# Attention's order and copy engines, and the queues of the feed-forward loads, in a transformer layer on 8 cores

## The chip, the cores and the metric

One Trainium2 chip, all 8 NeuronCores. Each core has TensorE (PE, matmuls), VectorE (DVE), ScalarE (ACT), GpSimd and SyncE (SP); SP and ACT also issue DMAs. The metric is the device time in microseconds (us) of the slowest core for the whole kernel. Each core computes its own 1024 rows of the result, with no exchange between cores.

## The reference

Attention with 16 query heads and 4 key/value heads, RMS-normed q and k, a causal mask, residual and layer norm, then a gated feed-forward layer, again with residual and layer norm. x is (2, 4096, 2048) in fp32, the hidden size is 8192.

```python
q = (x @ Wq).reshape(b, s, 16, 128)
k = (x @ Wk).reshape(b, s, 4, 128)
v = (x @ Wv).reshape(b, s, 4, 128)
q = _rmsnorm(q, q_gamma); k = _rmsnorm(k, k_gamma)      # k, v repeated for 4 heads each
scores = einsum('bqhd,bkhd->bhqk', q, k) * 128 ** -0.5   # causal mask
out = einsum('bhqk,bkhd->bqhd', softmax(scores), v).reshape(b, s, 2048) @ Wo
y = _layernorm(x + (out + x))
gate = einsum('bsd,hd->bsh', y, w_gate)
up = einsum('bsd,hd->bsh', y, w_up)
z = einsum('bsh,dh->bsd', silu(gate) * up, w_down)
result = _layernorm(y + z)
```

## The kernel before

A core takes one of the two sequences and every fourth tile of 128 rows of it, 8 tiles in all (NT = 8, slot g). The kernel runs in stages: K and V of all 4096 positions, Q of the core's rows, attention, output projection with layer norm, feed-forward, last layer norm. Engines run their own queues in program order and wait for each other by semaphores (`wt` is a wait, `tick` an increment; `sch` and `vch` also make the engine wait for its own instruction).

**Attention.** There are 8 x 16 iterations i, one for each slot g and head h. Slot g sees nb = g + 1 chunks of 512 keys. An iteration has four parts:

- `emit_stats(i)`: for each chunk one score matmul on PE into one of two PSUM tiles `pss` (L426), copied by ACT into `scr` (L432).
- `emit_sm_front(i)`: DVE masks the last chunk (L441) and takes the row maximum of all of them (L444).
- `emit_sm_back(i)`: ACT takes exp over all chunks into `ph`, with the row sum (L457); DVE takes the reciprocal (L462) and scales `ph` (L463).
- `emit_tav(i)`: for each chunk q4, PE transposes four blocks of `ph` into one of two tiles `pst` (L484), an engine EV copies them to `pt4` (L501 on ACT, L505 on DVE), and PE multiplies them with V into `pso` (L512). EV is ACT for even i and DVE for odd i. The transposes of chunk q4 + 1 are emitted ahead of the copy of q4, and the copy waits for them (L498); behind the last chunk stands a dummy transpose (L497). At the end EV copies `pso` into `zT` (L522, L526).

The loop emits front(i+1), back(i), stats(i+2), tav(i); ahead of it stand stats(0), stats(1) and front(0). At the first head of a slot ACT issues the load of the next slot's mask.

**Feed-forward.** The hidden size is done in 64 steps eht = 8 e8 + ht, eight to a block. A step multiplies the 1024 rows with 128 columns of the gate weights (L740, L743, 32 matmuls) and of the up weights (L750, L753, 32 matmuls). ACT applies SiLU to the gate (L760), DVE multiplies it with up (L764). After eight steps follow 256 down matmuls (L775), added into `f` by DVE (L786).

Weights come in fp32 and are cast. `issue_w(eht)` issues 32 loads of 64 KB, 16 into `wgs32` (L712) and 16 into `wus32` (L716), all from SP, into one of two buffers; SP waits for the cast of two steps before. `issue_w(eht + 1)` is called at the head of step eht. ACT casts both (L733, L734). The down weights of a step, 1 MB, are loaded into the single buffer `wds` (L730), issued by ACT, and cast by DVE into `wd16` (L767) behind the multiplication. The head of a step in the kernel before:

```python
if eht + 1 < 64:
    issue_w(eht + 1)
wt(SE, ve, wd_cast)
wd_rd = swd.tick(
    SE.dma_start(wds[:], wdT_d[128 * eht:128 * (eht + 1), :]))
wt(SE, swgu[p], w_rd[p])
wt(SE, te, w16_used[p])
SE.copy(wgs16[p][:], wgs32[p][:])
w_cast[p] = se.tick(SE.copy(wus16[p][:], wus32[p][:]))
```

Of the kernel before, what the change touches and what calls it, by code (L numbers as in the profile page):

```python
# [34 lines left out]
def build_program():  # L35
# [25 lines left out]
    def wt(eng, sem, val):  # L61
        if val <= 0:
            return
        key = (id(eng), id(sem))
        if wait_memo.get(key, 0) < val:
            eng.wait_ge(sem.h, val)
            wait_memo[key] = val
# [13 lines left out]
    with ExitStack() as ctx0:  # L81
        e0 = ctx0.enter_context
        te = Sem(nc, ctx0, "te")
        ve = Sem(nc, ctx0, "ve")
# [20 lines left out]
        with ExitStack() as ctxY, ExitStack() as ctxZ, ExitStack() as ctxA:  # L105
# [282 lines left out]
            with ExitStack() as c3:  # L388
# [29 lines left out]
                def emit_stats(i):  # L418
                    g, h = it_gh(i)
                    nb = g + 1  # L420
                    rho = i % 2
                    g4 = h // 4
                    for kb in range(nb):
                        p = kb % 2
                        wt(TE, se, sc[p])
                        mm = TE.matmul(pss[p][:], qT[:, h, 128 * g:128 * (g + 1)],  # L426
                                       kT[:, g4, 512 * kb:512 * (kb + 1)],
                                       start=True, stop=True)
                        mmd = te.tick(mm)
                        wt(SE, te, mmd)  # L430
                        wt(SE, ve, ve_scr_done[rho])
                        sc[p] = se.tick(SE.copy(scr[rho][:, 512 * kb:512 * (kb + 1)],  # L432
                                                pss[p][:]))

                def emit_sm_front(i):
                    g, h = it_gh(i)
                    nb = g + 1
                    rho = i % 2
                    wt(VE, se, max(sc))
                    wt(VE, sdm[g % 2], dm_ready[g % 2])  # L440
                    vch(VE.tensor_tensor(scr[rho][:, 512 * g:512 * (g + 1)],  # L441
                                         scr[rho][:, 512 * g:512 * (g + 1)],
                                         dmb[g % 2][:], op=OP.min))
                    nm_done[rho] = vch(VE.tensor_reduce(nm[rho][:],  # L444
                                                        scr[rho][:, 0:512 * nb],
                                                        axis=AX, op=OP.max, negate=True))
                    ve_scr_done[rho] = nm_done[rho]
                    dm_used[g % 2] = nm_done[rho]

                def emit_sm_back(i):  # L450
                    g, h = it_gh(i)
                    nb = g + 1
                    rho = i % 2
                    wt(SE, ve, nm_done[rho])
                    wt(SE, ve, li_done[rho])
                    wt(SE, te, te_ph_done[rho])
                    exp_done = sch(SE.activation(ph[rho][:, 0:512 * nb],  # L457
                                                 scr[rho][:, 0:512 * nb],
                                                 ACT.Exp, bias=nm[rho][:],
                                                 accum_out=ell[rho][:]))  # L460
                    wt(VE, se, exp_done)
                    li_done[rho] = vch(VE.reciprocal(li[rho][:], ell[rho][:]))  # L462
                    ex_done[rho] = vch(VE.tensor_scalar(ph[rho][:, 0:512 * nb],  # L463
                                                        ph[rho][:, 0:512 * nb],
                                                        li[rho][:, 0:1], 0.0,
                                                        op0=OP.mult, op1=OP.add))

                def emit_tav(i):
                    g, h = it_gh(i)
                    nb = g + 1  # L470
                    rho = i % 2
                    g4 = h // 4
                    EV = SE if (i % 2 == 0) else VE
                    evs = se if (i % 2 == 0) else ve
                    wt(TE, ve, ex_done[rho])
                    wt(TE, se if zev_eng[rho] == 0 else ve, zev_done[rho])

                    def emit_tchunk(q4):
                        pp = q4 % 2
                        wt(TE, se, se_pt_done[pp] if se_pt_eng[pp] == 0 else 0)  # L480
                        wt(TE, ve, se_pt_done[pp] if se_pt_eng[pp] == 1 else 0)
                        tr = None
                        for u in range(4):
                            tr = TE.transpose(pst[pp][:, 128 * u:128 * (u + 1)],  # L484
                                              ph[rho][:, 512 * q4 + 128 * u:
                                                       512 * q4 + 128 * (u + 1)], id16[:])
                        return te.tick(tr)

                    tch = [0] * (nb + 1)
                    tch[0] = emit_tchunk(0)  # L490
                    av_done = 0
                    for q4 in range(nb):
                        if q4 + 1 < nb:
                            tch[q4 + 1] = emit_tchunk(q4 + 1)
                        else:
                            tch[q4 + 1] = te.tick(
                                TE.transpose(pjk3[:], id16[:], id16[:]))  # L497
                        wt(EV, te, tch[q4 + 1])  # L498
                        if EV is SE:
                            se_pt_done[q4 % 2] = evs.tick(  # L500
                                SE.copy(pt4[q4 % 2][:], pst[q4 % 2][:]))  # L501
                            se_pt_eng[q4 % 2] = 0
                        else:
                            se_pt_done[q4 % 2] = evs.tick(
                                VE.tensor_copy(pt4[q4 % 2][:], pst[q4 % 2][:]))  # L505
                            se_pt_eng[q4 % 2] = 1
                        wt(TE, se if se_pt_eng[q4 % 2] == 0 else ve,
                           se_pt_done[q4 % 2])
                        av = None
                        for u in range(4):  # L510
                            ktile = 4 * q4 + u
                            av = TE.matmul(pso[rho][:],  # L512
                                           vsb[:, ktile, 128 * g4:128 * (g4 + 1)],
                                           pt4[q4 % 2][:, 128 * u:128 * (u + 1)],
                                           start=(ktile == 0),
                                           stop=(ktile == 4 * nb - 1))
                        av_done = te.tick(av)
                    te_ph_done[rho] = te.n
                    wt(EV, te, av_done)
                    if EV is SE:  # L520
                        zev_done[rho] = evs.tick(
                            SE.copy(zT[:, h, 128 * g:128 * (g + 1)], pso[rho][:]))  # L522
                        zev_eng[rho] = 0
                    else:
                        zev_done[rho] = evs.tick(
                            VE.tensor_copy(zT[:, h, 128 * g:128 * (g + 1)], pso[rho][:]))  # L526
                        zev_eng[rho] = 1
# [7 lines left out]
                for i in range(NIT):  # L535
                    g, h = it_gh(i)
                    if h == 0 and g + 1 < NT and dm_issued < g + 1:
                        pn = (g + 1) % 2
                        wt(SE, ve, dm_used[pn])
                        dm_ready[pn] = sdm[pn].tick(  # L540
                            SE.dma_start(dmb[pn][:], dmask_d[g + 1]))
                        dm_issued = g + 1
                    if i + 1 < NIT:
                        emit_sm_front(i + 1)
                    emit_sm_back(i)
                    if i + 2 < NIT:
                        emit_stats(i + 2)
                    emit_tav(i)
            zev_all = se.n
            ctxA.close()  # L550

# [129 lines left out]
            with ExitStack() as c5m:  # L681
# [24 lines left out]
                def issue_w(eht):  # L706
# [3 lines left out]
                    for dc in range(16):  # L710
# [2 lines left out]
                                         wgT_d[128 * dc:128 * (dc + 1),  # L713
                                               128 * eht:128 * (eht + 1)]))
                        r = swgu[p].tick(
                            SY.dma_start(wus32[p][:, dc, :],  # L716
                                         wuT_d[128 * dc:128 * (dc + 1),
                                               128 * eht:128 * (eht + 1)]))
                    w_rd[p] = r
# [2 lines left out]
                for e8 in range(8):  # L722
                    for ht in range(8):
                        eht = 8 * e8 + ht
                        p = eht % 2
                        if eht + 1 < 64:
                            issue_w(eht + 1)
                        wt(SE, ve, wd_cast)
                        wd_rd = swd.tick(
                            SE.dma_start(wds[:], wdT_d[128 * eht:128 * (eht + 1), :]))  # L730
                        wt(SE, swgu[p], w_rd[p])
                        wt(SE, te, w16_used[p])
                        SE.copy(wgs16[p][:], wgs32[p][:])  # L733
# [182 lines left out]
```

How the kernel before makes its waits and increments, by code:

```python
    def tick(self, instr, k=1):  # L29
        self.n += k * self.step
        instr.then_inc(self.h, k * self.step)
        return self.n
# [28 lines left out]
    def wt(eng, sem, val):  # L61
        if val <= 0:
            return
        key = (id(eng), id(sem))
        if wait_memo.get(key, 0) < val:
            eng.wait_ge(sem.h, val)
            wait_memo[key] = val
```

## Time and profile before

| | |
|---|---|
| median of 2 runs | 5664.69 us (5649.74 to 5679.64) |
| profiled execution | 5473.53 us |
| its span, slowest core | 5472.3 us |
| spans of the other cores | 5440.4 to 5465.0 us |
| PE matmul busy | 3427.8 us (63%) |
| ACT busy | 1412.4 us (26%) |
| DVE busy | 1305.9 us (24%) |
| chain that ended last, by engine | PE 58%, ACT 16%, DVE 14% |

All times in the profile are of one execution on the slowest core. "Idle before" a group is the time its engine stood still directly ahead of its instructions, with the instruction that released it. The granted clock is TensorE's, as a share of 2.4 GHz. A DMA's row on SPq or ACTq is its issue on the queue of that engine, not the transfer.

### The profile page before, as it was taken

The numbers are of one execution on the slowest core, as the hardware profiler recorded it, in microseconds if no ns is written. First come the engines' busy times: TensorE is split into PE (matmuls) and PEld (weight loads), VectorE is DVE, ScalarE is ACT, GpSimd is POOL, SyncE is SP. The second block draws the span as 40 slices with busy tenths as digits, with TensorE's granted clock in tenths as the row PEclk, the third lists the DMA queues.
The fourth block names the chain that finished last, engine by engine and source line by source line (L and its number), as shares of the span: only waits on it lengthen the run. The fifth ranks groups of instructions, "written<-read, shape, count | busy, mean of one in ns | idle before, by whom it ended". The sixth has DMA issues, their size and how long they took to land.

```text
span 5472.3 us, 43357 instructions; the slowest of 8 cores (5440.4 to 5472.3 us)
## 1 busy us (share of the span) xinstructions
PE 3427.8 (63%) x15152; PEld 1619.8 (30%) x15152; DVE 1305.9 (24%) x1799; ACT 1412.4 (26%) x2525; POOL 0.2 (0%) x4
## 2 busy tenths in 40 slices
PE   3565567677545555555555435577878788787872
PEld 1222223233222333333333212233323333232331
DVE  1111100000244443334333323111212112121216
ACT  1222211212344444444444301111111111112111
POOL 0000000000000000000000000000000000000000
PEclk8676677888655555555555567788989889898986
DMA  3111121121000000000000030443242423424221
GB/s 110 47 53 54 49 68 46 49 80 48 26 4 3 1 3 2 1 3 1 1 0 1 20 134 31 118 120 106 87 134 87 137 86 103 120 88 137 87 71 62
DMA packets 343077, 325.20 MB, mean 59 GB/s; under 512 B 38224, under 2 KB 300496, under 8 KB 326480
## 3 DMA queue, kind: packets, MB, share of 16 engines
q1 hardware_dynamic: 311760, 177.71, 11.7%
q10 hardware_dynamic: 31104, 144.72, 7.9%
q8 instruction: 126, 2.06, 0.2%
q14 instruction: 87, 0.71, 0.0%
HBM read 313.88 MB, written 8.39 MB: 59 GB/s over the span
## 4 chain that ended last, share of the span: by engine, by line
PE 58%; ACT 16%; DVE 14%; issue 7%; DMA 3%; ACTq 1%; DVEq 0%; SPq 0%
PE psd L775 8%; PE psq L323 8%; PE pso L512 6%; PE psg L740 5%; PE psg L743 5%; PE pst L484 5%; PE psu L753 4%; PE psu L750 4%; ACT pt L501 3%; DVE nm L444 3%; PE psk L221 3%; ACT ph L457 3%; PE psv L223 3%; DVE pt L505 2%; PE pswo L615 2%
## 5 line engine op out<-in xcount | busy, mean ns | idle before, releaser
L740 PE MATMUL psg<-yT,wgs 128*128 128x512 f16 x1024 | 469.1, 458 | 404.6 <-ACT wus L734 404.6
L512 PE MATMUL pso<-pt,vsb 128*128 128x128 f16 x2304 | 336.1, 299 | 432.8 <-ACT pt L501 237.5
L323 PE MATMUL psq<-wqs,xqs 128*128 128x512 f32 x1024 | 486.5, 638 | 44.5 <-DMA xqs<-xqT 40.2
L775 PE MATMUL psd<-wd,gatedT 128*128 128x512 f16 x2048 | 455.0, 386 | 20.9 <-DVE wd L767 20.9
L743 PE MATMUL psg<-yT,wgs 128*128 128x512 f16 x1024 | 466.4, 456 | 0.0
L484 PE MATMUL pst<-id,ph 128*128 128x128 f16 x2304 | 336.3, 310 | 178.8 <-DVE ph L463 178.8
L426 PE MATMUL pss<-kT,qT 128*128 128x512 f16 x576 | 311.1, 604 | 195.9 <-ACT scr L432 194.9
L432 ACT COPY scr<-pss 128x512 f32<-128x512 f32 x576 | 312.4, 587 | 405.0 <-PE pss L426 395.8
L753 PE MATMUL psu<-yT,wus 128*128 128x512 f16 x1024 | 388.2, 379 | 0.0
L750 PE MATMUL psu<-yT,wus 128*128 128x512 f16 x1024 | 388.1, 379 | 0.0
L764 DVE TENSOR_TENSOR gatedT<-gsil,psu 128x1024 f16<-128x1024 f16 x64 | 78.1, 1221 | 1298.1 <-PE psu L753 1298.1
L512 PEld LDWEIGHTS pso<-pt,vsb 128*128 128x128 f16 x2304 | 199.7, 126 | 569.3 <-issue 569.3
L444 DVE TENSOR_REDUCE nm<-scr 128x1 f32<-128x512 f32 (+7 forms) x128 | 326.8, 2553 | 13.9 <-DVE scr L441 0.9
L484 PEld LDWEIGHTS pst<-id,ph 128*128 128x128 f16 x2304 | 254.5, 144 | 233.9 <-issue 231.3
L760 ACT ACTIVATE gsil<-psg 128x1024 f16<-128x1024 f32 x64 | 65.5, 1023 | 958.6 <-PE psg L743 958.6
L323 PEld LDWEIGHTS psq<-wqs,xqs 128*128 128x128 f32 x1024 | 202.5, 204 | 322.7 <-issue 322.1
L740 PEld LDWEIGHTS psg<-yT,wgs 128*128 128x128 f16 x1024 | 117.1, 114 | 596.6 <-issue 522.2
L457 ACT ACTIVATE ph<-scr,nm 128x512 f16<-128x512 f32 (+7 forms) x128 | 283.9, 2218 | 0.0
L775 PEld LDWEIGHTS psd<-wd,gatedT 128*128 128x128 f16 x2048 | 202.8, 99 | 273.1 <-issue 39.9
L501 ACT COPY pt<-pst 128x512 f16<-128x512 f16 x288 | 168.5, 585 | 443.3 <-PE pst L484 373.5
L733 ACT CAST wgs<-wgs 128x2048 f16<-128x2048 f32 x64 | 121.4, 1897 | 568.4 <-DVE wd L767 551.0
L221 PE MATMUL psk<-wkv,xTt 128*128 128x512 f16 x512 | 237.3, 463 | 38.8 <-ACT xTt L211 38.8
(107 smaller groups left out, 2684.5 us busy)
## 6 DMA issues: line engine op xcount, KB each, us to landing
wgs<-wgT SPq DMA_DIRECT2D x1024, 64.0 KB, 2.0
wds<-wdT ACTq DMA_DIRECT2D x64, 1024.0 KB, 4.9
wus<-wuT SPq DMA_DIRECT2D x1024, 64.0 KB, 2.0
xr<-x ACTq DMA_DIRECT2D x32, 1024.0 KB, 5.8
wqs<-wq SPq DMA_DIRECT2D x64, 256.0 KB, 3.1
wqs<-wq ACTq DMA_DIRECT2D x64, 256.0 KB, 3.1
wos<-wo SPq DMA_DIRECT2D x16, 1024.0 KB, 6.4
xqs<-xqT ACTq DMA_DIRECT2D x32, 256.0 KB, 7.9
```

The source lines that it names most:

```text
L221: TE.matmul(psk[p][:], lhsT, wkv[:, dc, 0:512], start=(dc == 0), stop=(dc == 15))
L323: mq = TE.matmul(psq[j][:], xqs[:, dc, 128 * j:128 * (j + 1)], wqs[dc % 2][:], start=(dc == 0), stop=(dc == 15))
L444: nm_done[rho] = vch(VE.tensor_reduce(nm[rho][:], scr[rho][:, 0:512 * nb], axis=AX, op=OP.max, negate=True))
L457: exp_done = sch(SE.activation(ph[rho][:, 0:512 * nb], scr[rho][:, 0:512 * nb], ACT.Exp, bias=nm[rho][:], accum_out=ell[rho][:]))
L484: tr = TE.transpose(pst[pp][:, 128 * u:128 * (u + 1)], ph[rho][:, 512 * q4 + 128 * u: 512 * q4 + 128 * (u + 1)], id16[:])
L501: SE.copy(pt4[q4 % 2][:], pst[q4 % 2][:]))
L512: av = TE.matmul(pso[rho][:], vsb[:, ktile, 128 * g4:128 * (g4 + 1)], pt4[q4 % 2][:, 128 * u:128 * (u + 1)], start=(ktile == 0), stop=(kti ...
L740: mg = TE.matmul(psg[:, 0:512], wgs16[p][:, dc, :], yT[:, dc, 0:512], start=(dc == 0), stop=(dc == 15))
L743: mg = TE.matmul(psg[:, 512:1024], wgs16[p][:, dc, :], yT[:, dc, 512:1024], start=(dc == 0), stop=(dc == 15))
L750: mup = TE.matmul(psu[:, 0:512], wus16[p][:, dc, :], yT[:, dc, 0:512], start=(dc == 0), stop=(dc == 15))
L753: mup = TE.matmul(psu[:, 512:1024], wus16[p][:, dc, :], yT[:, dc, 512:1024], start=(dc == 0), stop=(dc == 15))
L775: md = TE.matmul(psd[:, 512 * dout:512 * (dout + 1)], gatedT[:, ht2, 128 * tt:128 * (tt + 1)], wd16[:, ht2, 512 * dout:512 * (dout + 1)], ...
```

## The change

Three things are changed.

1. In attention the loop emits tav(i-1) at the head of iteration i, ahead of front(i+1), back(i) and stats(i+2), and the last tav behind the loop. A name `rho3` is brought in for the index of `scr`; it is i % 2, as `rho` is.
2. In `emit_tav` the engine that copies a chunk alternates by (i + q4) % 2 instead of by i % 2. The copy into `zT` stays by i % 2.
3. In the feed-forward stage the loads of `wus32` are issued by ACT instead of SP, and the load of `wds` is issued by SP for even eht and by ACT for odd eht.

The diff, without the lines that only rename `rho` to `rho3`:

```diff
@@ emit_sm_front, emit_sm_back, emit_stats @@
+                    rho3 = i % 2
...
@@ emit_tav @@
-                        wt(EV, te, tch[q4 + 1])
-                        if EV is SE:
-                            se_pt_done[q4 % 2] = evs.tick(
+                        EVq = SE if (i + q4) % 2 == 0 else VE
+                        evq = se if (i + q4) % 2 == 0 else ve
+                        wt(EVq, te, tch[q4 + 1])
+                        if EVq is SE:
+                            se_pt_done[q4 % 2] = evq.tick(
                                 SE.copy(pt4[q4 % 2][:], pst[q4 % 2][:]))
                             se_pt_eng[q4 % 2] = 0
                         else:
-                            se_pt_done[q4 % 2] = evs.tick(
+                            se_pt_done[q4 % 2] = evq.tick(
                                 VE.tensor_copy(pt4[q4 % 2][:], pst[q4 % 2][:]))
                             se_pt_eng[q4 % 2] = 1
@@ loop over i @@
                         dm_issued = g + 1
+                    if i >= 1:
+                        emit_tav(i - 1)
                     if i + 1 < NIT:
                         emit_sm_front(i + 1)
                     emit_sm_back(i)
                     if i + 2 < NIT:
                         emit_stats(i + 2)
-                    emit_tav(i)
+                emit_tav(NIT - 1)
@@ issue_w @@
                         r = swgu[p].tick(
-                            SY.dma_start(wus32[p][:, dc, :],
+                            SE.dma_start(wus32[p][:, dc, :],
                                          wuT_d[128 * dc:128 * (dc + 1),
                                                128 * eht:128 * (eht + 1)]))
@@ loop over ht @@
                         if eht + 1 < 64:
                             issue_w(eht + 1)
-                        wt(SE, ve, wd_cast)
+                        Qd = SY if eht % 2 == 0 else SE
+                        wt(Qd, ve, wd_cast)
                         wd_rd = swd.tick(
-                            SE.dma_start(wds[:], wdT_d[128 * eht:128 * (eht + 1), :]))
+                            Qd.dma_start(wds[:], wdT_d[128 * eht:128 * (eht + 1), :]))
```

## Rows read from the trace of the kernel before

**Rows 1.** Stretches: us, then busy PE, PEld, DVE, ACT, POOL; clock, DMA share, GB/s.

```profile
1414.00:3121.00 1707.00, 887.37 (x5267) 510.10 (x5267) 675.07 (x863) 794.19 (x1244) 0.00 (x0) 0.50 0.01 2
3454.60:5361.00 1906.40, 1481.27 (x6148) 632.40 (x6149) 327.12 (x384) 303.39 (x194) 0.00 (x0) 0.87 0.36 106
```

**Rows 2.** Costliest groups: busy us, mean ns | idle before, released by.

```profile
L740 PE MATMUL psg<-yT,wgs 128*128 128x512 f16 x1024 | 469.1, 458 | 404.6 <-ACT wus L734 404.6
...
L457 ACT ACTIVATE ph<-scr,nm 128x512 f16<-128x512 f32 (+7 forms) x128 | 283.9, 2218 | 0.0
...
L733 ACT CAST wgs<-wgs 128x2048 f16<-128x2048 f32 x64 | 121.4, 1897 | 568.4 <-DVE wd L767 551.0
```

**Rows 3.** Timelines of ACT, PE, DVE, one feed-forward step: start us, us, instruction [idle before].

```profile
3976.56 1.02 ACT L760 ACTIVATE gsil<-psg 128x1024 f16<-128x1024 f32 x1 [9.38 <-PE psg L743]
...
3982.99 0.38 PE L753 MATMUL psu<-yT,wus 128*128 128x512 f16 x1
...
3984.61 1.22 DVE L767 CAST wd<-wds 128x2048 f16<-128x2048 f32 x1
...
3986.34 1.90 ACT L733 CAST wgs<-wgs 128x2048 f16<-128x2048 f32 x1 [8.76 <-DVE wd L767]
...
3990.18 0.58 PE L740 MATMUL psg<-yT,wgs 128*128 128x512 f16 x1 [6.82 <-ACT wus L734]
```

**Rows 4.** Chain that ended last, attention, g = 7: start us, us, what.

```profile
2788.83 0.59 ACT pt L501
...
2790.66 0.59 ACT pt L501
...
2801.34 0.59 ACT pt L501
...
2802.91 3.81 ACT ph L457 x2
...
2812.43 0.44 DVE pt L505
...
2814.11 0.44 DVE pt L505
...
2825.39 0.69 DVE scr L441
...
2832.48 0.58 PE pst L484 x4
```

**Rows 5.** Timelines of PE and DVE in the same stretch.

```profile
2811.26 1.06 PE L484 MATMUL pst<-id,ph 128*128 128x128 f16 x8
...
2823.93 0.42 DVE L505 COPY pt<-pst 128x512 f16<-128x512 f16 x1 [0.94 <-PE pjk L497]
```

**Rows 6.** Groups by shape in attention, nb = 2.

```profile
L444 DVE TENSOR_REDUCE nm<-scr 128x1 f32<-128x1024 f32 x16 | 19.5, 1220 | 1.6
...
L457 ACT ACTIVATE ph<-scr,nm 128x1024 f16<-128x1024 f32 x16 | 18.5, 1156 | 0.0
```

**Rows 7.** Timeline of SP's queue, feed-forward: first and last of 14 issues.

```profile
3975.69 0.43 SPq L712 DMA_DIRECT2D wgs<-wgT  x1
...
3981.86 0.43 SPq L716 DMA_DIRECT2D wus<-wuT  x1
```

**Rows 8.** Timeline of ACT and its queue, K/V stage and Q stage.

```profile
86.38 0.27 ACT L258 COPY kT<-ptk 128x128 f16<-128x128 f16 x1 [1.46 <-PE pjk L254]
86.46 0.33 ACTq L185 DMA_DIRECT2D xr<-x  x1
...
1091.41 9.07 ACTq L309 DMA_DIRECT2D xqs<-xqT  x15
```

**Rows 9.** Stretches as in rows 1: a gate, start of down matmuls, Q stage.

```profile
4013.55:4023.30 9.75, 9.75 (x33) 3.82 (x34) 0.00 (x0) 0.00 (x0) 0.00 (x0) 0.70 0.46 127
4125.11:4128.50 3.39, 3.39 (x9) 1.19 (x10) 0.00 (x0) 3.02 (x2) 0.00 (x0) 0.51 0.66 213
849.00:904.00 55.00, 54.73 (x104) 23.03 (x104) 0.00 (x0) 0.00 (x0) 0.00 (x0) 0.81 0.21 62
```

More of the change, by code:

```diff
@@ L420, in emit_stats @@
                     nb = g + 1
-                    rho = i % 2
+                    rho3 = i % 2
                     g4 = h // 4
@@ L430, in emit_stats @@
                         wt(SE, te, mmd)
-                        wt(SE, ve, ve_scr_done[rho])
-                        sc[p] = se.tick(SE.copy(scr[rho][:, 512 * kb:512 * (kb + 1)],
+                        wt(SE, ve, ve_scr_done[rho3])
+                        sc[p] = se.tick(SE.copy(scr[rho3][:, 512 * kb:512 * (kb + 1)],
                                                 pss[p][:]))
@@ L438, in emit_sm_front @@
                     rho = i % 2
+                    rho3 = i % 2
                     wt(VE, se, max(sc))
                     wt(VE, sdm[g % 2], dm_ready[g % 2])
-                    vch(VE.tensor_tensor(scr[rho][:, 512 * g:512 * (g + 1)],
-                                         scr[rho][:, 512 * g:512 * (g + 1)],
+                    vch(VE.tensor_tensor(scr[rho3][:, 512 * g:512 * (g + 1)],
+                                         scr[rho3][:, 512 * g:512 * (g + 1)],
                                          dmb[g % 2][:], op=OP.min))
                     nm_done[rho] = vch(VE.tensor_reduce(nm[rho][:],
-                                                        scr[rho][:, 0:512 * nb],
+                                                        scr[rho3][:, 0:512 * nb],
                                                         axis=AX, op=OP.max, negate=True))
-                    ve_scr_done[rho] = nm_done[rho]
+                    ve_scr_done[rho3] = nm_done[rho]
                     dm_used[g % 2] = nm_done[rho]
@@ L453, in emit_sm_back @@
                     rho = i % 2
+                    rho3 = i % 2
                     wt(SE, ve, nm_done[rho])
@@ L457, in emit_sm_back @@
                     exp_done = sch(SE.activation(ph[rho][:, 0:512 * nb],
-                                                 scr[rho][:, 0:512 * nb],
+                                                 scr[rho3][:, 0:512 * nb],
                                                  ACT.Exp, bias=nm[rho][:],
```

## Prediction

> **What bounds the kernel now.** I read the table of stretches first [rows 1]. Attention (1414 to 3121 us) is 1707 us with PE busy 887 and the granted clock at 0.50 throughout (1.2 GHz); no engine is near full, so a chain of dependent steps sets it. The feed-forward stage is 1906 us with PE busy 1481: matmuls set it, and the holes between them. Next the costliest groups [rows 2]: the largest hole is L740, the first gate matmul, which sat 404.6 us behind the ACT cast of L734. ACT's first cast (L733) in turn sat 551.0 us behind the DVE cast of L767.
>
> The timelines of one feed-forward step say why [rows 3]. Count from the start of SiLU, 3976.56. Up matmuls end at 3982.99 + 0.38 = 3983.37 (+6.81). DVE multiplies, then casts wds until 3984.61 + 1.22 = 3985.83 (+9.27). ACT has waited for that, because its next instruction is the load into wds. It issues it, casts from 3986.34 (+9.78), and the next gate starts at 3990.18 (+13.62), 6.82 after the up matmuls. The hole stands before ht = 1 to 7 of each block, 56 times; the weights of ht = 0 are cast under the down matmuls.
>
> In attention I followed the chain of waits over a pair of iterations at g = 7 [rows 4]. The even one repeats: ACT copy, four AV matmuls, four transposes, next ACT copy, 1.83 us apart (2788.83, 2790.66). The odd one does the same with DVE, 1.68 apart (2812.43, 2814.11). Between them I count from the end of the last copy. After the even one (2801.34 + 0.59 = 2801.93) exp starts 0.98 later, since the zT copy after the AV matmuls is ahead of it on ACT; then come exp and the score copies and matmuls, and the next transposes start at 2811.26 [rows 5]: 9.33. After the odd one (2823.93 + 0.42 = 2824.35 [rows 5]) DVE's mask starts at 2825.39, then reduction and scale, and the next transposes at 2832.48: 8.13. These two ways are 8.35 from exp's start and 7.09 from the mask's.
>
> **The change, part by part.** *Renaming.* rho3 equals rho; the same instructions come out. Nothing.
>
> *Moving emit_tav.* Before, iterations run front(i+1), back(i), stats(i+2), tav(i); after, tav(i-1), front(i+1), back(i), stats(i+2). Written out, these are one sequence cut at another place, with the last tav added behind the loop. Every engine's order stays. Only the load of dmask, 8 in all, goes ahead of a tav on ACT's queue, in front of a copy that waits for transposes anyway; a single issue took 0.33 [rows 8]. At most 8 x 0.33 = 3 us if it were not hidden; I take nothing.
>
> *Alternating the copies.* The copy of chunk q4 waits for the transposes of q4 + 1, and the transposes of q4 + 2 are queued on PE behind the AV matmuls of q4, which wait for that copy. So two copies never overlap, whichever engines do them. A pair of iterations still holds as many ACT as DVE pitches, 3.51 for two. Bounds: all 448 pitches behind a first chunk at 1.68, or all at 1.83, in place of their mean: -33 to +33 us; I take 0.
>
> What loses its cover is the rest: exp ran under odd iterations (their copies were DVE's), DVE's mask and reduction under even ones. Both now come behind the copies. For nb = 8: the odd iteration's last copy is now ACT's, and its zT copy is DVE's, so exp starts at once and ACT's way ends 8.35 after the copy, DVE's old way 8.13: 0.22 longer. The even iteration's last copy is now DVE's, which starts the mask at once: 7.09, hidden under ACT's 9.33 by 2.2. At smaller even nb ACT's way shrinks faster than DVE's after odd iterations; at odd nb the engine in question has its last copy a chunk earlier. The barest cover is after even ones at nb = 2, where exp + 0.85 must outlast reduction + 0.72: 1.16 + 0.85 = 2.01 against 1.22 + 0.72 = 1.94 [rows 6]. Sum: 8 x 0.22 = +2 us.
>
> *wds by turns from SP and ACT.* For even eht ACT no longer waits for DVE; for odd eht it does. Even steps with a hole are ht = 2, 4, 6 in 8 blocks: 24; odd ones 32. SP's wait for wd_cast stands behind its 16 loads of wgs(eht+1), which have been issued by then, and ahead of those of wgs(eht+2), which can't start before this step's casts anyway. The load starts at the same moment as now and is wanted a whole step later. Nothing late.
>
> *wus from ACT.* This decides. ACT now issues 16 DMAs between SiLU and the casts, in every step. No row shows 64 KB loads in a run on ACT. SP's start 6.17 / 13 = 0.474 apart (first and last of 14) [rows 7]. ACT's loads of xqs are 9.07 / 15 = 0.605 apart [rows 8], but they are 256 KB each, 433 GB/s, where the transfers could be the limit; SP's run at 138 GB/s. I take 0.474; the range keeps 0.605. A DMA starts while ACT computes, 0.08 after the start of a copy [rows 8]. So the 16 run from +0.10 to 0.10 + 16 x 0.474 = +7.7. Odd steps: ACT then waits until +9.27 as before; this costs nothing and has 1.6 us to spare (issues up to 0.573). Even steps: the casts start at +7.7 instead of +9.78, 2.1 us each: 24 x 2.1 = -50 us. SP's own 16 start with the gate and end 7.6 later, before ACT's. By the Trainium skill (Advanced Engine Details and Errata, "Clock Domains") the SP and ACT sequencers run at one clock; by that ACT's pitch is SP's and the sum is the same. No run here shows it yet.
>
> The Trainium skill (DMA: Bandwidth & Descriptors, "Issuing engines are not separate DMA queues") says that starting DMAs on several engines saves only the time to start them, usually small. By that rule alone the move of wus would change nothing. Here the issues are 15.2 us a step on SP, where they are hidden, and the half that moves to ACT takes most of what the freed wait gives.
>
> *Clock.* A gate behind a hole begins at 0.50; the one at 4013.55 had 0.70 over 9.75 us for what the up matmuls do in 6.9 [rows 9], so up to 2.9 lost. The hole of even steps falls to 4.7 us. A hole of 2.61, before the down matmuls at 4125.11, was followed by 0.51 too, so I take no gain. Bound: 24 x 2.9 = -70.
>
> *Start of the stage.* ACT issues 32 DMAs ahead of its first cast where SP issued 32 whose landing it awaited: nothing.
>
> **Sum.** 5472.3 - 50 + 2 = 5424 for the span of this execution. It took 5473.53 in all; the median of the two runs is 5664.69, 191 longer. The trace shows a level of 0.81 under long matmul stretches [rows 9]. At it the 6.9 us of up matmuls become 8.5, the wait for DVE ends 1.6 later, and an even step gains 3.7: 89 us in all. How much of the 191 is that isn't shown; between 50 and 89 I take 65: 5664.7 - 65 = 5600 us.
>
> **Rivals.**
> *A. ACT issues slower.* For: the xqs loads [rows 8]. Against: they are four times as large. At 0.605 an even step gains nothing and the casts of an odd one come 0.4 later: 32 x 0.4 = +14, 5679 us; each 0.05 more costs 16 x 56 x 0.05 = 45. Over 2% (113 us) from 0.72. Chance 0.10.
> *B. Slower, attention.* The exp of odd iterations, once hidden, adds to the gap behind them: half of 283.9 [rows 2] = +142, less the 65: 5742 us. It decides where exp and score copies outlast DVE's way by more than a little. Against: the reduction is as long as exp or longer from nb = 2 on [rows 6], and the mask comes on top. Chance 0.07.
> *C. The whole hole goes* in 24 steps, the issues being so short (under 0.2) that issues and casts fit under the up matmuls: 24 x (6.8 + 2.9) = -233: 5432 us. Against: the pitch of rows 7. Chance 0.05.
> *D. Copies on two engines overlap*, and a pitch falls by a copy's 0.5: 448 x 0.5 = -224: 5441 us. Against: PE's order, above. Chance 0.04.
>
> **How the numbers follow.** The forecast, a gain of about 1%, has 0.74. A measurement of this kernel tells about 2% from no change: 5551 to 5778. Faster takes C, D and 0.01 of the forecast's low side: 0.10. Slower takes the far parts of A and B, where issues pass 0.72 or both costs add up: 0.10. Same: 0.80. The low end, 5555, has most of the clock's 70 or the 33 of attention; the high end, 5690, has 0.605 on ACT, or +33 with nothing from 0.81.
>
> **What would show it.** ACT's queue behind SiLU: 16 issues, 0.474 apart, the last done at +7.7. The hole before the gate: 4.7 us for ht = 2, 4, 6, and 6.8 for the odd. L733 waits for L767 only 32 times. In attention the same starts of chunks and gaps, with exp no longer under the copies. It is wrong if ACT's pitch differs, if the gate's slow stretch goes, or if a gap in attention moves by over 1 us.

## The result, and the profile after

| | before | changed |
|---|---|---|
| median | 5591.84 us (5451.77 to 5737.63, 10 runs) | 5514.41 us (5388.62 to 5669.48, 11 runs) |
| ratio | | 0.9883, 95% interval 0.9835 to 0.993 |

The kernel became 1.2% faster. The forecast said a gain of about 1% (5600 / 5664.69 = 0.9886), by the mechanism that the profile then showed, but gave it as 5600 us, from 5555 to 5690, and the time measured is 5514.

In some executions of either kernel some cores are granted a clock of 0.81 in long matmul stretches and the kernel takes up to 5% longer; the ratio above and, unless it is said otherwise, the stage times below leave these out.

Attention is cut here from the first score matmul to the first load of the output projection's weights, feed-forward from the first load of `wgs32` to the first transpose of the last layer norm. In the profiled execution of the changed kernel core 3 kept the full clock in both (span 5394.1 us). Its stretches of attention and of feed-forward, columns as in [rows 1]:

```profile
1413.20:3115.20 1702.00, 891.98 (x5312) 515.14 (x5312) 671.49 (x864) 783.59 (x1185) 0.00 (x0) 0.50 0.01 2
...
3431.00:5282.60 1851.60, 1476.38 (x6145) 630.43 (x6146) 327.17 (x384) 303.66 (x193) 0.00 (x0) 0.89 0.38 109
```

Cut at the same instructions, the kernel before has 1700.0 us of attention and 1906.1 of feed-forward on its core 0 (its eight cores: 1699.6 to 1701.2, and 1906.1 to 1909.6). So on these cores attention took 2 us more and feed-forward 54.5 less. The waits of the feed-forward stage (engine, line, waited for: us in total, times, longest) name the holes, which are the times PE stands still ahead of a gate. They came to 404.6 us [rows 2] and are now 354.8. Where ACT had waited 551.0 us for DVE alone [rows 2], there are now 32 waits for DVE and 32 in which it waited for nothing but its own queue:

```profile
PE psg L747 <- ACT wus L741: 354.8, 57, 20.7
ACT wgs L740 <- DVE wd L774: 277.6, 32, 9.0
...
ACT wgs L740 <- issue: 224.6, 32, 15.4
```

And the timeline of ACT and its queue over an even and an odd step:

```profile
3939.20 1.03 ACT L767 ACTIVATE gsil<-psg 128x1024 f16<-128x1024 f32 x1 [9.32 <-PE psg L750]
3939.22 7.73 ACTq L722 DMA_DIRECT2D wus<-wuT  x16
3947.04 1.90 ACT L740 CAST wgs<-wgs 128x2048 f16<-128x2048 f32 x1 [6.81 <-issue]
3948.85 1.89 ACT L741 CAST wus<-wus 128x2048 f16<-128x2048 f32 x1
3959.79 1.02 ACT L767 ACTIVATE gsil<-psg 128x1024 f16<-128x1024 f32 x1 [9.05 <-PE psg L750]
3959.81 7.54 ACTq L722 DMA_DIRECT2D wus<-wuT  x16
3969.09 0.34 ACTq L737 DMA_DIRECT2D wds<-wdT  x1
3969.52 1.90 ACT L740 CAST wgs<-wgs 128x2048 f16<-128x2048 f32 x1 [8.71 <-DVE wd L774]
```

The 16 issues begin 0.02 us after the start of SiLU and last 7.5 to 7.7 us in most steps (9.1 at most). In the even step the first cast follows them, 7.84 after SiLU here (7.7 in most); in the odd step ACT is through with them after 7.56 and then waits for DVE until 9.3, as in [rows 3].

### The profile page after: what moved, and what is told of

Its sections match the earlier page's. It is cut to its first block, busy times and chain, and to the rows that moved or that the text cites. A ratio compares the mean times of both kernels' runs of the same rounds, so it can differ in the third digit from the quotient of the medians.

```text
span 5554.5 us, 43304 instructions; the slowest of 8 cores (5394.1 to 5554.5 us)
## 1 busy us (share of the span) xinstructions
PE 3590.1 (65%) x15152; PEld 1656.2 (30%) x15152; DVE 1300.9 (23%) x1799; ACT 1413.6 (25%) x2525; POOL 0.2 (0%) x4
## 4 chain that ended last, share of the span: by engine, by line
PE 57%; ACT 17%; DVE 13%; issue 7%; ACTq 4%; DMA 2%; DVEq 0%; SPq 0%
PE psd L782 10%; PE psq L323 8%; PE psg L747 6%; PE pso L516 6%; PE psg L750 6%; PE pst L486 5%; ACT ph L459 4%; ACTq L722 3%; PE psu L760 3%; PE psu L757 3%; ACT pt L505 3%; PE psk L221 3%; PE psv L223 3%; DVE nm L445 2%; PE pswo L621 2%
## 5 line engine op out<-in xcount | busy, mean ns | idle before, releaser
L747 PE MATMUL psg<-yT,wgs 128*128 128x512 f16 x1024 | 493.5, 482 | 328.0 <-ACT wus L741 328.0
L782 PE MATMUL psd<-wd,gatedT 128*128 128x512 f16 x2048 | 533.0, 433 | 20.9 <-DVE wd L774 20.9
L750 PE MATMUL psg<-yT,wgs 128*128 128x512 f16 x1024 | 490.7, 479 | 0.0
L323 PE MATMUL psq<-wqs,xqs 128*128 128x512 f32 x1024 | 461.1, 612 | 38.2 <-DMA xqs<-xqT 37.2
L760 PE MATMUL psu<-yT,wus 128*128 128x512 f16 x1024 | 432.4, 422 | 0.0
L757 PE MATMUL psu<-yT,wus 128*128 128x512 f16 x1024 | 432.3, 422 | 0.0
L782 PEld LDWEIGHTS psd<-wd,gatedT 128*128 128x128 f16 x2048 | 220.8, 108 | 333.2 <-issue 293.9
L509 DVE COPY pt<-pst 128x512 f16<-128x512 f16 x288 | 122.3, 425 | 821.2 <-PE pst L486 658.2
```

Of the source, the lines that this page charges most:

```text
L323: mq = TE.matmul(psq[j][:], xqs[:, dc, 128 * j:128 * (j + 1)], wqs[dc % 2][:], start=(dc == 0), stop=(dc == 15))
L747: mg = TE.matmul(psg[:, 0:512], wgs16[p][:, dc, :], yT[:, dc, 0:512], start=(dc == 0), stop=(dc == 15))
L750: mg = TE.matmul(psg[:, 512:1024], wgs16[p][:, dc, :], yT[:, dc, 512:1024], start=(dc == 0), stop=(dc == 15))
L757: mup = TE.matmul(psu[:, 0:512], wus16[p][:, dc, :], yT[:, dc, 0:512], start=(dc == 0), stop=(dc == 15))
L760: mup = TE.matmul(psu[:, 512:1024], wus16[p][:, dc, :], yT[:, dc, 512:1024], start=(dc == 0), stop=(dc == 15))
L782: md = TE.matmul(psd[:, 512 * dout:512 * (dout + 1)], gatedT[:, ht2, 128 * tt:128 * (tt + 1)], wd16[:, ht2, 512 * dout:512 * (dout + 1)], ...
```

## Experiments: which part made the difference

Stage times, us, each kernel on one core at the full clock. Cores of one execution differ by 2 to 4 us in attention and, in the kernels with regular holes, by up to 3.5 us in feed-forward; with wds always from SP they differ by 14 us or more:

| kernel | attention | feed-forward |
|---|---|---|
| before | 1700.0 | 1906.1 |
| changed | 1702.0 | 1851.6 |
| feed-forward part alone | 1701.4 | 1851.6 |
| attention part alone | 1702.5 | 1909.7 |
| wus from ACT alone | 1700.5 | 1902.7 |
| wds by turns alone | 1699.4 | 1691.1 |
| whole change, wus issued behind the casts | 1701.2 | 1684.3 |
| whole change, wus as one DMA | 1702.5 | 1687.7 |
| wds always from SP | 1699.5 | 1458.6 |
| same, one DMA each for wgs and wus | 1701.9 | 1380.1 |
| transposes one chunk further ahead | 1262.4 | 1906.2 |
| same, copies alternating | 1266.7 | 1909.5 |

**The feed-forward part alone.** The attention of before, the queues of the change.

```diff
-                            SY.dma_start(wus32[p][:, dc, :],
+                            SE.dma_start(wus32[p][:, dc, :],
...
-                        wt(SE, ve, wd_cast)
+                        Qd = SY if eht % 2 == 0 else SE
+                        wt(Qd, ve, wd_cast)
```

> The change without its attention part: wus from ACT, wds by turns, attention as before. My theory: all of the gain is here. ACT's first cast starts 7.7 us after SiLU in even steps and 9.7 in odd ones, the hole before the gate is 4.7 us for ht = 2, 4, 6 and 6.8 for ht = 1, 3, 5, 7; the feed-forward stage falls from 1906 us to 1850 to 1875, the ratio to before is 0.988 to 0.992, as for the whole change. Rival, that the attention part brings some of it: a ratio nearer to 0.995.

Feed-forward took 1851.6 us on seven cores and 1855.0 on one, the same as in the whole change. The whole times (5389.24 to 5549.8 us in 4 runs, before 5593.91 to 5787.73 in 7) spread too widely for the ratio that was expected. The stage carries the verdict: all the gain is here.

**The attention part alone.** The reverse.

> The change without its feed-forward part. My theory: the moved tav is the same sequence and the copies never overlap, so the attention stage takes 1702 us instead of 1700 (0.2 us more for each of 8 pairs at nb = 8), ratio 1.000. Rival B, exp loses its cover: attention 1840 us, ratio 1.025. Rival D, copies overlap: attention near 1475 us, ratio 0.96.

```profile
1397.60:3100.10 1702.50, 892.84 (x5312) 515.87 (x5312) 671.58 (x864) 782.24 (x1185) 0.00 (x0) 0.50 0.01 2
```

This stretch is attention on core 2: 1702.5 us, and 1700.8 to 1702.9 over the eight cores, against 1699.6 to 1701.2. Rivals B and D are out. From the starts of DVE's reductions, a pair of iterations takes 23.48 us at nb = 4 and 34.11 at nb = 6 in both kernels, and at nb = 8 44.9 instead of 44.7 in the mean of the cores. That is the 0.2 of the sum.

The stage alone would not show so little: kernels with the attention of before reach 1702.3 us on single cores. Cut in two it does. The time from the start of the first to that of the last copy into `pt4`, summed over the 128 iterations, is 752.5 us before and 752.1 here; the rest of the stage is 948.0 and 949.6. That rest lies between 947.7 and 948.3 us on every core of the six kernels with the old attention, and between 949.3 and 950.1 with the changed one. So the copies cost the same, and what lost its cover costs 1.6 us.

**wus from ACT alone.**

> Only the loads of wus go to ACT; wds stays on ACT in every step. My theory: the 16 issues end 7.7 us after SiLU, before DVE's cast at 9.27, so they are hidden in all steps: casts start at 9.7 to 9.8, holes 6.8, feed-forward 1906 us, ratio 1.000. Rival, that fewer issues on SP bring loads earlier and with them time: feed-forward below 1890. Rival A, that issues on ACT are dear: casts later than 9.8 and feed-forward above 1920.

1902.7 us on cores 4 to 7, with casts 9.8 us after SiLU and holes of 6.8 in nearly all steps. That is 3.4 us less than before. Of it 1.3 is a shorter wait before the first gate of the stage (21.3 us instead of 22.6); the rest was not followed up, and cores of the kernel before differ by as much (1906.1 and 1909.6). Under DVE's wait the 7.6 us of issues are hidden.

**wds by turns alone.** wus stays on SP.

> Only wds goes by turns; wus stays on SP. My theory: without 16 issues between SiLU and the casts ACT casts about 1 us after SiLU's start in even steps, done 4.9 after it, under the 6.8 us of up matmuls, so the hole before ht = 2, 4, 6 is gone and with it the gate's slow start: 24 x (6.8 + 2.5) = 220 us, feed-forward near 1690 us, ratio 0.96. Then the move of wus costs the change some 160 us of what the freed wait gives. Rival: SP's 32 issues (15.2 us) behind its wait for DVE bring the weights late, and the hole only changes its releaser: feed-forward above 1800, ratio 0.98 or more.

ACT's timeline on core 6, an even step and the next SiLU, and the stretch of the stage:

```profile
3922.50 1.02 ACT L761 ACTIVATE gsil<-psg 128x1024 f16<-128x1024 f32 x1 [9.80 <-PE psg L744]
3923.42 1.89 ACT L734 CAST wgs<-wgs 128x2048 f16<-128x2048 f32 x1
3925.21 1.90 ACT L735 CAST wus<-wus 128x2048 f16<-128x2048 f32 x1
3936.36 1.02 ACT L761 ACTIVATE gsil<-psg 128x1024 f16<-128x1024 f32 x1 [9.26 <-PE psg L744]
```

```profile
3414.70:5105.80 1691.10, 1430.32 (x6144) 621.80 (x6145) 327.11 (x384) 299.97 (x193) 0.00 (x0) 0.90 0.41 120
```

The casts follow SiLU at once, the hole is gone, and so is the slow start of the gate: SiLU to SiLU is 13.86 us here and 23.24 in the step before (from 3899.26). 1906.1 - 1691.1 = 215 us, as worked out (220). So wds by turns is worth 215 us, and wus from ACT, ahead of the casts, takes 160 of it away again (1851.6 - 1691.1).

**The same 16 loads behind the casts.** The whole change, with the issues at another place:

```diff
+                def issue_wu(eht):
...
                         w_cast[p] = se.tick(SE.copy(wus16[p][:], wus32[p][:]))
+                        if eht + 1 < 64:
+                            issue_wu(eht + 1)
```

> The whole change, but ACT issues the 16 loads of wus for the next step behind the two casts of a step instead of ahead of them. My theory: it is only their place between SiLU and the casts that costs. Casts of even steps start 0.9 us after SiLU, the holes of ht = 2, 4, 6 go, feed-forward 1691 us as with wus on SP; attention 1702. Rival, that 1024 more DMAs on ACT cost wherever they stand: feed-forward above 1750.

ACT and its queue on core 4:

```profile
3910.00 5.77 ACTq L727 DMA_DIRECT2D wus<-wuT  x12
3921.59 1.02 ACT L775 ACTIVATE gsil<-psg 128x1024 f16<-128x1024 f32 x1 [9.81 <-PE psg L758]
3921.77 0.82 ACTq L727 DMA_DIRECT2D wus<-wuT  x2
3922.51 1.89 ACT L746 CAST wgs<-wgs 128x2048 f16<-128x2048 f32 x1
3922.61 1.90 ACTq L727 DMA_DIRECT2D wus<-wuT  x4
...
3924.55 4.80 ACTq L727 DMA_DIRECT2D wus<-wuT  x10
```

1684.3 us. The 16 issues of the step are 2 + 4 + 10; those of the step before ended at 3915.77. The first two, at 3921.77, run while SiLU computes and the casts that stand ahead of them in the program have not started. So ACT's queue went on to the DMAs without waiting for those casts to start. With the same DMAs on the same queue the stage takes 1851.6 us when they stand in front of the casts and 1684.3 when they stand behind them: it is their place. One thing was not foreseen: the kernel beats wus on SP (1691.1) by 7. Of this 6 are at the start of the stage, where the wait before the first gate is 15.8 us instead of 22.0.

**One DMA in place of 16.** The whole change, at the old place:

```diff
-                    for dc in range(16):
...
+                    r = swgu[p].tick(
+                        SE.dma_start(wus32[p][:],
+                                     wuT_d[:, 128 * eht:128 * (eht + 1)].rearrange(
+                                         "(c p) n -> p c n", p=128)))
```

> The whole change, but the 16 loads of wus of a step are one DMA of 1 MB from ACT, at the same place. My theory: one issue holds ACT for 0.4 us instead of 7.6, casts of even steps start 1 us after SiLU, feed-forward near 1691 us. Rival, that a long DMA holds the queue that issues it for several us (as the wus issues from SP did, 4 to 6 us each, when they came right behind a wgs of 1 MB): casts of even steps later than 4 us after SiLU, feed-forward above 1720.

ACT on core 1:

```profile
3904.94 1.02 ACT L767 ACTIVATE gsil<-psg 128x1024 f16<-128x1024 f32 x1 [9.36 <-PE psg L750]
3904.95 0.37 ACTq L722 DMA_DIRECT2D wus<-wuT  x1
3905.86 1.89 ACT L740 CAST wgs<-wgs 128x2048 f16<-128x2048 f32 x1
```

One issue of 1 MB, in 2048 rows of 512 bytes, took 0.37 us (the median of 64 as well), no more than one of 64 KB; feed-forward 1687.7 us (1691.1 on others). What cost the 160 us was the number of DMAs issued there. A long DMA right behind another is a different case, as the kernel with one DMA each for wgs and wus shows below.

## Experiments: how far the two ideas go

**wds always from SP**, wus on SP too (`Qd = SY`).

> As wds by turns, but wds comes from SP in every step, wus from SP too; attention as before. My theory: the wait of ACT for DVE was all that made the holes. All 56 go, and SP's queue becomes the bound of a step: 32 issues at 0.474 and one for wds are 15.6 us against 13.8 of gate and up matmuls. Feed-forward 8 x (57.1 + 2.6) + 8 x 13.8 + 56 x 15.7 + 20 = 1487 us, so 1460 to 1520 on an undisturbed die. Rival, that SP behind its wait for DVE falls back further and weights come late: above 1560, with holes of 3 us or more.

ACT on core 0, and the stretch of the stage:

```profile
4035.65 1.02 ACT L761 ACTIVATE gsil<-psg 128x1024 f16<-128x1024 f32 x1 [9.20 <-PE psg L744]
4038.07 1.90 ACT L734 CAST wgs<-wgs 128x2048 f16<-128x2048 f32 x1 [1.39 <-DMA wus<-wuT]
...
4049.47 1.02 ACT L761 ACTIVATE gsil<-psg 128x1024 f16<-128x1024 f32 x1 [7.70 <-PE psg L744]
4053.96 1.90 ACT L734 CAST wgs<-wgs 128x2048 f16<-128x2048 f32 x1 [3.47 <-DMA wus<-wuT]
```

```profile
3417.90:4876.50 1458.60, 1358.33 (x6145) 604.82 (x6146) 329.43 (x384) 301.07 (x193) 0.00 (x0) 0.97 0.48 139
```

1458.6 us (1451.1 to 1466.0 over the cores), less than the 1487 expected and just under the low end given, 1460. From the second block on the holes of ht = 1 to 4 are gone; from ht = 5 the casts wait for the loads, and holes of 0 to 3.5 us come back (1.9 to 2.8 in the median). SP is the bound only in the second half of a block, since what it issued under the down matmuls carries the first half; the sum had charged it in all steps.

**The same with one DMA each for wgs and wus.**

> As wds from SP, and the 16 loads of wgs of a step are one DMA of 1 MB, those of wus another (same 512-byte rows): 2 issues instead of 32. My theory: if the cost is per issue, SP is free and a step is bound by its matmuls, 13.8 us: feed-forward 8 x 59.7 + 64 x 13.8 + 20 = 1381 us where the clock stays at 1.00. Rival, that the cost is per row described (2048 rows of 512 bytes in each DMA either way): one issue lasts about 7.6 us and the stage takes as long as with 32, near 1487.

```profile
3422.20:4802.30 1380.10, 1342.14 (x6145) 603.66 (x6146) 327.13 (x384) 297.51 (x193) 0.00 (x0) 0.98 0.56 147
```

SP's queue on the same core, one step:

```profile
3623.48 0.34 SPq L730 DMA_DIRECT2D wds<-wdT  x1
3623.91 0.39 SPq L711 DMA_DIRECT2D wgs<-wgT  x1
3624.34 4.00 SPq L715 DMA_DIRECT2D wus<-wuT  x1
```

1380.1 us against 1381 worked out, with PE busy for 1342; the six cores at the full clock lie between 1376.2 and 1390.4, so the agreement to 1 us is chance. A second DMA of 1 MB right behind the first does hold its queue: 4.0 us here, 6.3 in the median of the 64 and 11.4 at most. On SP nothing urgent stands behind it. So the issue of a large DMA is short only where no other large one stands directly ahead of it; what the second waits for isn't shown.

**Transposes one chunk further ahead.** The attention of before, with a third `pst`; in `emit_tav` the transposes of q4 + 2 come ahead of the AV matmuls of q4, and the copy into `pt4` waits for the AV matmuls of q4 - 2:

```diff
+                    emit_next(0)
+                    emit_next(1)
...
                     for q4 in range(nb):
-                        if q4 + 1 < nb:
-                            tch[q4 + 1] = emit_tchunk(q4 + 1)
...
+                        emit_next(q4 + 2)
```

> The kernel before with a third pst tile: the transposes of chunk q4 + 2 go ahead of the AV matmuls of q4 on PE, so the copy of q4 + 1 need not wait for those of q4; copies stay on one engine per iteration. My theory: PE's order was what kept the copies apart. A pitch falls from 1.76 to 0.9 to 1.0 us (four transposes and four AV matmuls at 1.2 GHz are 0.86), 448 x 0.8 = 360 us, attention near 1340 us. Rival: the copy and its waits bound a pitch in any order, attention above 1600 us.

The chain in an even iteration at g = 7, and the stretch of attention:

```profile
2555.08 0.58 PE pso L522 x4
2555.66 0.43 PE pst L484 x4
2556.09 0.43 PE pso L522 x4
2556.52 0.43 PE pst L484 x4
...
2558.87 0.59 ACT pt L512
```

```profile
1404.80:2667.20 1262.40, 734.51 (x5312) 465.89 (x5312) 674.27 (x864) 776.37 (x1185) 0.00 (x0) 0.69 0.01 2
```

In the middle of the iteration the copies have left the chain: PE goes from AV to transposes without a wait, 0.86 us a chunk. The first copy and the last two are still in it. The stage took 438 us less, more than the 360 expected. From copy to copy the chunks took 752 us in all before and 332 here, or 1.68 and 0.74 each (core 0); the rest of the stage gives 17. 0.74 is less than the 0.86 that four transposes and four AV matmuls take at 1.2 GHz: the expectation had priced PE at that level throughout, and the granted clock rose from 0.50 to 0.69. How the surplus divides between the clock and the order isn't shown.

**The same, copies alternating.**

> As the kernel with the third pst tile, but copies alternate between ACT and DVE by (i + q4) % 2 as in the change. My theory: PE already bounds a pitch with one engine, so alternating gains nothing more here either, and exp and DVE's reduction lose their cover: attention within 1340 to 1370 us, equal to or up to 20 us over the kernel with one engine. Rival D in this order: two engines overlap their copies, attention 40 us or more below that kernel.

```profile
1394.20:2660.90 1266.70, 747.43 (x5312) 468.21 (x5312) 671.46 (x864) 785.43 (x1185) 0.00 (x0) 0.66 0.01 2
```

1263.8 to 1267.7 us over the cores against 1262.4 to 1265.8, or 2 us more in the mean. The expected level was missed as in the last kernel, the comparison held, but not only for the reason given. From copy to copy the chunks take 322 us in the mean of the cores, 10 less than with one engine (333), so PE was not all of the bound there. The rest of the stage takes 944 us instead of 931: exp and DVE's reduction lose their cover. The two cancel.

**Together.** Third `pst`, wds from SP, one DMA each for wgs and wus.

> What helped, together: the third pst tile with transposes one chunk further ahead (copies on one engine per iteration), wds from SP, wgs and wus as one DMA each from SP. My theory: the stages don't touch each other, so attention 1263 us and feed-forward 1380 us stay, 4475 us on an undisturbed die, ratio to before 0.82. Rival: the longer busy stretches lower the clock (0.81) and feed-forward is above 1440 on all cores, ratio 0.84 or more.

Core 3, and the feed-forward stretch of core 0:

```profile
1399.40:2659.80 1260.40, 731.01 (x5312) 463.72 (x5312) 674.17 (x864) 775.94 (x1185) 0.00 (x0) 0.69 0.01 2
...
2973.30:4349.60 1376.30, 1336.72 (x6144) 602.63 (x6145) 327.04 (x384) 297.07 (x193) 0.00 (x0) 0.99 0.56 147
```

```profile
2983.60:4405.10 1421.50, 1345.08 (x6145) 602.11 (x6146) 327.48 (x384) 300.69 (x193) 0.00 (x0) 0.98 0.55 142
```

Median 4517.6 us (4485.78 to 4755.96, 4 runs), with 5635.31 (5449.2 to 5775.73, 7 runs) for before beside it. The lowest times of both give 0.823, without an interval. On core 3 the two gains add up as expected (span 4461.4 us, where 4475 was worked out). The other cores took 4485.8 to 4516.8, with up to 45 us more in feed-forward at nearly the same clock. On core 0 the casts of ht = 4 to 7 come up to 6.4 us after SiLU, 3.7 in the mean, instead of 0.9. They wait for the weights: 39 waits for the loads of wus, 126.6 us in all, against 7 and 25.9 on core 3, and from issue to landing such a load takes 21.4 us in the median against 15.7. So here the arrival of the weights bounds these steps; why they are slower on one core than on another isn't shown.

## Why the prediction was right and where it was wrong

**The moved tav and the renaming: right.** They were put at nothing, and the kernel with the attention part alone leaves nothing for them beside the 1.6 us below. They were not run by themselves.

**Alternating: right.** +2 us worked out for what loses its cover, +1.6 measured as the rest of the stage, and 0 for the copies, where 752.5 us became 752.6 (means of the eight cores). The chain of the changed kernel on core 3 shows the pitches mixed, 3.52 us for one of ACT and one of DVE, where [rows 4] give 1.83 + 1.68:

```profile
2811.96 0.60 ACT pt L505
...
2813.81 0.44 DVE pt L509
...
2815.48 0.60 ACT pt L505
```

The experiments with a third `pst` confirm the reason, PE's order: with that order changed the copies drop out of most of the chain, and only then do two engines gain on the copies (10 us).

**wds by turns and wus from ACT: right.** Even casts come at +7.7 and odd ones at +9.7, and the pitch is 7.54 / 16 = 0.47 on ACT as on SP. That agrees with the one clock that the Trainium skill (Advanced Engine Details and Errata, "Clock Domains") gives for both sequencers. The holes are 4.7 us before most of ht = 2, 4, 6 and 6.8 before the others. The sum was 50 us; the shorter holes of the even steps gave 48.3. The stage gave 54.5, since two terms that the prediction put at nothing were small gains: 1.9 at the start of the stage (22.6 us before the first gate, now 20.7), and 3.7 in the gates, which from first gate matmul to SiLU took 592.7 us in all before and 589.0 after. Cores 0 and 1 show 1872.6 us; core 0 had 0.81 in place of 1.00 in the last 150 us of the stage. Rival A is out, by the pitch of 0.47 (why the xqs loads stood 0.605 apart isn't shown), and so is C, by the 7.7 us. What C priced at 233 us was had at 215 as soon as the issues stood elsewhere.

The Trainium skill's rule that starting DMAs on several engines saves only the starting time (DMA: Bandwidth & Descriptors, "Issuing engines are not separate DMA queues") agrees with the kernel with wus from ACT alone, which changed 3.4 us. The starting time is paid by the engine that gets it; in front of the casts that was 160 us here.

**The clock: right.** Behind the holes of 4.7 us the gates take 8.8 to 9.5 us, behind those of 6.8 they take 9.1 to 9.9, and behind no hole 7.2. So the slow start stayed, as the prediction said. Behind shorter holes it is not certain: with wds from SP, on core 0, one hole of 2.34 us was followed by the full clock and another by 0.52.

**The saving at 0.81: right in kind.** On core 6, which had 0.81 for most of this stage, the odd step casts at +11.23 and the even one at +7.69, a gain of 3.5 us where 3.7 was worked out. The 89 us for all even steps have no counterpart, since the trace of before has no core with this level in the stage. The steps on core 6:

```profile
3959.30 1.02 ACT L767 ACTIVATE gsil<-psg 128x1024 f16<-128x1024 f32 x1 [11.10 <-PE psg L750]
...
3970.53 1.90 ACT L740 CAST wgs<-wgs 128x2048 f16<-128x2048 f32 x1 [10.20 <-DVE wd L774]
...
3984.45 1.02 ACT L767 ACTIVATE gsil<-psg 128x1024 f16<-128x1024 f32 x1 [10.23 <-PE psg L750]
...
3992.14 1.90 ACT L740 CAST wgs<-wgs 128x2048 f16<-128x2048 f32 x1 [6.67 <-issue]
```

**The step that failed** is the first term of the last sum, "5664.7 - 65 = 5600". Every saving was set against 5664.69, the median of two runs. Over ten runs the median of before is 5591.84, 73 us less, and single ones lie between 5451.77 and 5737.63. The working had seen that the profiled execution was 191 us shorter than that median, and had put that down in part to the level of 0.81. It used this to raise the saving from 50 to 65 us, but not to ask how often the level comes, nor to widen the range: its ends, 5555 and 5690, held only the doubts about the change. Those doubts were the small part. The forecast's ratio on the base that was measured later gives 0.9886 x 5591.84 = 5528, and 5514.41 is within 0.3% of it. That closeness is in part luck: 15 of the 65 us stand for the level of 0.81, and the measured ratio of 0.9883 leaves such executions out. For the others the working gives 5424 / 5472.3 = 0.991, also inside the interval. And the base moves with the executions that happen to be drawn: three later sets of before (7, 3 and 7 executions) have medians of 5635.8, 5636.1 and 5635.3 us, on which the forecast's ratio gives some 5571, inside the range. A range that took in the profiled 5473 as a possible base, less 50, would have started at about 5420 and held the result. How much of the two first runs was that level can't be said, as they have no record of the clock; that it can go with 190 us is shown by the cores of one execution (wus from ACT alone), die 0 with it and die 1 without (cores 0 to 3 are die 0). Of the 200 us between cores 3 and 4, 82 are in feed-forward (1985.1 and 1902.7 us):

```profile
core 3: 5624.9 us, clock 0.683
core 4: 5424.8 us, clock 0.718
```

## What to carry to other kernels

A DMA issued by a compute engine costs that engine its issue time, so count the issues between a release and the work that waits, and put them behind that work or make them one large DMA (not two in a row); the same 16 loads cost 160 us in one place and nothing in another. A wait for another engine's result in front of a load holds all that is queued behind it: moving the load to a queue with nothing urgent behind it was the whole gain here. When two engines share a chain of short steps, look first for the program order on the third engine that keeps the steps apart, because dividing them brings nothing while it stands, and afterwards only what isn't lost again where work had run under them (10 us gained and 12 lost here). And when the profiled execution is 3% from the median, the base belongs into the range.

## What the runs showed that was not expected

- The clock of attention wasn't fixed: once PE went from AV matmuls to transposes without a wait, the granted clock of the stage went from 0.50 to 0.69. The gain was 438 us, where 360 had been priced at 1.2 GHz.
- A DMA of 1 MB in 2048 rows is issued in 0.37 to 0.39 us, like one of 64 KB, but the next one behind it held the queue for 6.3 us in the median (1.6 to 11.4).
- ACT's queue issues DMAs 0.02 us after the start of SiLU, and even 0.7 us before a cast starts that stands ahead of them in the program. Issuing overlaps computing ahead of it, but delays what comes behind.
